# Attention and mixture of experts on one core: the low half of each expert pair's gated product is subtracted on GpSimd instead of VectorE

## Reference

```python
x = layernorm(x + attention(x))     # 16 heads of 16, causal, window of 64
x = layernorm(x + moe(x))
...
g = einsum('th,eih->tei', x, gate_w)      # 16 experts of 128, 4 of them per token
u = einsum('th,eih->tei', x, up_w)
h = silu(g) * u                           # the gated product
yo = einsum('tei,ehi->teh', h, down_w)
routed = einsum('te,teh->th', combine, yo)
out = routed + shared                     # shared: the same MLP, 256 wide, for all tokens
```

## Time and profile before

| what | value |
|---|---|
| median of 3 runs | 1211.92 us (1211.19 to 1212.39) |
| the profiled execution's own time | 1207.38 us |
| its span | 1205.6 us |
| PE busy | 1001.5 us (83%) |
| DVE busy | 857.8 us (71%) |
| ACT busy | 628.5 us (52%) |
| POOL busy | 493.3 us (41%) |
| chain that ended last | PE 49%, DVE 18%, POOL 12%, issue 8%, DMA 5%, SPq 4%, ACT 3% |
| low half on DVE (L1431) | 136 instructions, 63.5 us |
| scatters, gathers on POOL | 128 and 128 instructions, 127.5 and 124.3 us |

### The profile page before, as it was taken

The page is one execution under the profiler, slowest core; times in us unless marked ns, Lnnn a source line. Parts: engine busy times, 40 slices in busy tenths (PEclk is TensorE's granted clock), DMA queues, the critical chain, the costliest instruction groups (busy, mean ns, idle before and its releaser), DMA issues.

```text
span 1205.6 us, 25555 instructions
## 1 busy us (share of the span) xinstructions
PE 1001.5 (83%) x8693; PEld 587.6 (49%) x8693; DVE 857.8 (71%) x1907; ACT 628.5 (52%) x1449; POOL 493.3 (41%) x712
## 2 busy tenths in 40 slices
PE   7976998989887999998899879887998787966950
PEld 3533433345432465555565445454655466845730
DVE  7666897778885667778777887787767659665443
ACT  4413776767444566664466556654565553324430
POOL 7922221133138112312463733213726726663334
PEclk9988998999888999999999899999999988978985
DMA  5843267421113343242285733322756644968952
GB/s 181 269 136 114 57 215 255 153 70 33 50 58 118 88 111 79 55 80 73 87 176 126 179 92 96 66 76 75 158 120 157 187 123 145 204 151 198 231 155 74
DMA packets 221978, 152.85 MB, mean 127 GB/s; under 512 B 139936, under 2 KB 199072, under 8 KB 221856
## 3 DMA queue, kind: packets, MB, share of 16 engines
q1 hardware_dynamic: 207936, 114.50, 37.9%
q0 software_dynamic: 12288, 33.57, 9.0%
q10 hardware_dynamic: 1632, 3.15, 1.0%
HBM read 50.36 MB, written 73.40 MB: 103 GB/s over the span
## 4 chain that ended last, share of the span: by engine, by line
PE 49%; DVE 18%; POOL 12%; issue 8%; DMA 5%; SPq 4%; ACT 3%; DVEq 0%; ACTq 0%; POOLq 0%
PE bank L711 12%; PE bank L566 10%; PE bank L537 8%; PE bank L550 8%; POOL a_pool L1023 5%; DVE a_mx L1203 5%; PE bank L724 4%; POOL rows L1015 3%; DMA a_pool<-outs,e_slot 2%; DVE e_R L1449 2%; SPq L801 2%; PE bank L540 2%; PE bank L736 2%; DVE e_ga L1420 1%; POOL p_qk L948 1%
## 5 line engine op out<-in xcount | busy, mean ns | idle before, releaser
L1203 DVE TENSOR_REDUCE a_mx<-bank 128x1 f32<-128x512 f32 (+3 forms) x720 | 424.4, 619 | 190.0 <-PE bank L540 115.6
L1084 ACT ACTIVATE a_PT<-bank 128x512 f32<-128x512 f32 (+4 forms) x832 | 374.1, 497 | 215.7 <-PE bank L550 212.9
L550 PE MATMUL bank<-a_QS,a_KS 113*128 113x512 f16 (+4 forms) x832 | 276.5, 340 | 34.4 <-DVE a_mx L1203 25.1
L973 POOL TENSOR_SCALAR_AFFINE_SELECT a_PT<-a_PT 128x256 f32<-128x256 f32 (+1 forms) x288 | 110.9, 392 | 432.6 <-ACT a_PT L1084 431.9
L537 PE MATMUL bank<-a_KS,a_QS 112*128 112x512 f16 (+4 forms) x832 | 265.7, 340 | 23.7 <-DMA a_KS<-k_dram 14.0
L566 PE MATMUL bank<-a_PT,a_VG 128*17 128x512 f32 (+4 forms) x1664 | 186.0, 520 | 18.5 <-POOL a_PT L973 18.5
L1023 POOL DMA_INDIRECT a_pool<-outs,e_slot x128 | 124.3, 971 | 84.8 <-issue 33.9
L1015 POOL DMA_INDIRECT rows<-e_XR,e_slot x128 | 127.5, 996 | 66.0 <-issue 35.4
L537 PEld LDWEIGHTS bank<-a_KS,a_QS 112*128 112x128 f16 x832 | 81.4, 100 | 126.1 <-ACT a_PT L1084 51.1
L550 PEld LDWEIGHTS bank<-a_QS,a_KS 113*128 113x128 f16 x832 | 82.3, 100 | 100.9 <-DVE a_mx L1203 40.8
L1149 ACT ACTIVATE e_tq<-bank 128x256 f32<-128x256 f32 x136 | 51.0, 382 | 145.6 <-PE bank L711 145.5
(11 more groups left out here) (156 smaller groups left out, 1263.2 us busy)
## 6 DMA issues: line engine op xcount, KB each, us to landing
outs<-e_ys SPq DMA_DIRECT2D x104, 256.0 KB
rows<-a_pool SPq DMA_DIRECT2D x48, 256.0 KB, 3.2
q_dram<-p_qk SPq DMA_DIRECT2D x32, 128.0 KB, 2.7
k_dram<-p_qk SPq DMA_DIRECT2D x32, 128.0 KB, 2.6
v_dram<-p_vs SPq DMA_DIRECT2D x8, 512.0 KB, 4.2
a_QS<-q_dram SPq DMA_DIRECT2D x64, 64.0 KB
a_KS<-k_dram SPq DMA_DIRECT2D x64, 64.0 KB
a_VG<-v_dram SPq DMA_DIRECT2D x16, 256.0 KB, 4.4
```

What stands on the lines that cost most here:

```text
L550: pe.matmul(ps[:, 0:(qc + 1) * CH - q0], KS[p][0:MR + 1, kt // NT, h % 2, kt % NT * P:kt % NT * P + P], QS[p][0:MR + 1, qc, h, q0 - qc * C ...
L973: pool.affine_select(out=a, in_=a, compare_op=ALU.is_ge, fill=0.0, base=q0 - (kt * P - WIN), pattern=[[0, 2], [1, w]], channel_multiplier= ...
L1084: act.activation(PT[(G + i) % 2][:, h, 0:w], bank("ST", G, i, h)[:, 0:w], ACT.Exp)\
L1203: dve.tensor_reduce(mx[:, piece, t // NT, heads[0]:heads[0] + n, t % NT], bank("S", G, u)[:, 0:n * w].rearrange("p (h k) -> p h k", h=n), ...
```

## The change

The job `hl` of each of the 136 pairs leaves DVE's list and enters POOL's, at the same half-slot `q + 3`. The instruction, its shape, its buffers, its waits and the semaphore it raises stay the same; what it stands behind and in front of is different.

```diff
--- before.py
+++ after.py
@@ -205,7 +205,7 @@
         act[q].append(("tanh", g, n))
         dve[q + 1].append(("gate", g, n))
         act[q + 2].append(("hh", g, n))
-        dve[q + 3].append(("hl", g, n))
+        pool[q + 3].append(("hl", g, n))
         if n >= NPS[g]:
             sp[q - (5 if q < tail + 10 else 10)].append(("load_rows", g, n))
             last[g] = y = put(("y", g, n), q + (5 if q < tail else 7))
@@ -1004,6 +1004,13 @@
                         on.wait_ge(f["row_hi"], c + 1)
                         pool.tensor_tensor(XR[:, j:j + NT, D:2 * D], x1_of(c), XR[:, j:j + NT, 0:D], op=ALU.subtract)\
                             .then_inc(f["row_lo"], 1)
+                    elif what == "hl":
+                        q = nth(*a)
+                        on.wait_ge(f["hh_done"], q + 1)
+                        if q >= NHB:
+                            on.wait_ge(*free_h(q - NHB))
+                        pool.tensor_tensor(hl[q % NHB][:], hf[q % NHF][:], hh[q % NHB][:], op=ALU.subtract)\
+                            .then_inc(f["hl_done"], 1)
                     elif what == "scatter":
                         b, t, k = a
                         on.wait_ge(f["slot_done"], b + 1)
@@ -1423,13 +1430,6 @@
                         on.wait_ge(f["hl_done"], q - NHF + 1)
                         dve.scalar_tensor_tensor(hf[q % NHF][:], ps[:, 2 * P:4 * P], 0.5 / WSC / WSC, ga[q % 2][:],
                                                  op0=ALU.mult, op1=ALU.mult).then_inc(f["h_done"], 1)
-                    elif what == "hl":
-                        q = nth(*a)
-                        on.wait_ge(f["hh_done"], q + 1)
-                        if q >= NHB:
-                            on.wait_ge(*free_h(q - NHB))
-                        dve.tensor_tensor(hl[q % NHB][:], hf[q % NHF][:], hh[q % NHB][:], op=ALU.subtract)\
-                            .then_inc(f["hl_done"], 1)
                     elif what == "add_shared":
                         b, n = a
                         c, tile = shared_place(b, n)
```

## The result

| | before | changed |
|---|---|---|
| median | 1211.56 us (4 runs, 1211.19 to 1212.39) | 1224.72 us (4 runs, 1217.70 to 1230.04) |
| ratio | | 1.0103, 95% interval 1.0062 to 1.0144 |
| the profiled execution's own time, its span | 1207.38, 1205.6 us | 1222.22, 1220.5 us |
| DVE, POOL busy | 857.8, 493.3 us | 814.6, 582.6 us |

The account below looks back on a forecast made before the run. PE was taken to bound half the chain, POOL's transfers the stretch behind the attention; -5 + 12 + 5 + 5 + 2 + 3 + 2 = +24 on 1207.38 gave 1231.4, plus 4.5 to the median: 1236 us, range 1216 to 1256.

Parts of the forecast that it names:

- relief of DVE: 136 subtractions leave DVE; only what lies on the chain counts: -5 us, between 0 and -10.
- scatters of group 1, of group 2: Six low halves each between masks, 4.8 us, less a cover of 2.7: +1.5 us each, +3 together (0 to 6).
- group 0's gathers: Five low halves on POOL, 4.0 us, half of it hidden: +2 us (0 to 4).
- group 1's gathers: Nine low halves between first and last gather, +7.2, partly taken by pauses for combines: +5 us (0 to 8).
- tail, to PE's product behind it: Low halves among group 3's and 4's scatters and group 2's gathers delay PE's next down product: +12 us (0 to 18).
- from there to the end (group 3's gathers): Nine low halves ahead of group 3's gathers and five between them, less pauses for combines: +5 us (2 to 8).
- meeting on SBUF: Low halves on POOL slow DVE's combines; if a sixth meets one in full: +2 us (0 to 10).
- The price of a low half: One low half on POOL takes 0.80 us (bounds 0.62 and 1.0), 109 us in all.
- Stretch from group 4's first scatter to the end of group 2's last gather: Behind the attention: some 79 us instead of 68; forecast wrong if it does not grow by at least 8.
- the third rival: Each stop feeds the next: POOL waits for high halves, late POOL stops DVE's gates; +16 in the tail, 1252 us, chance 0.15.
- the landing loops hide the gathers' share: Pauses for combines in the gather stretches absorb most low halves there: +8, 1220 us, chance 0.15.
- The relief deciding: POOL's landings hide every added low half; PE gains 6 us in the tail plus 5 of relief: 1201 us, chance 0.07.

Follow-up runs that it names:

- the two mirror kernels: Changed kernel with the low halves behind the attention back on VectorE: 1.0005 of the kernel before; with only those on GpSimd: 1.0093.
- the second trace: Profiled execution of the changed kernel run again with nothing edited: 1221.23 us (8 runs), 1.0087 of the kernel before.
- Narrow on GpSimd: Changed kernel with the subtraction cut from 256 to 16 columns in all but the first six pairs: 1203.04 us, 0.9937 of the kernel before.
- the free stretches: Kernel before with only 45 attention pairs' low halves on GpSimd, away from scatters and group 0's and 1's gathers: 1207.94 us, 0.9969.
- all four variants: Against the kernel before: low halves on GpSimd for scatters of groups 3 and 4, 0.9863; from group 2's gathers on, 0.9902; 16 columns on GpSimd, 0.9773; on VectorE, 0.9942.

## Why the prediction was right, and where it was too large

By its own steps, each against the changed kernel's trace (starts from the table):

| step | forecast | shown by the trace |
|---|---|---|
| relief of DVE | -5 | -7.5 |
| scatters of group 1, of group 2 | +1.5, +1.5 | +3.6, +1.4 |
| group 0's gathers | +2 | +1.4 |
| group 1's gathers | +5 | +2.5 |
| tail, to PE's product behind it | +12 | +10.1 |
| from there to the end (group 3's gathers) | +5 | +3.3 |
| meeting on SBUF | +2 | within the others |
| sum | +24 | +14.85 in this trace; 10.5 and 13 by the medians |

The relief is what is left: at group 3's first scatter the kernel was 1.42 late, the four stretches of the attention had cost 8.9, so the rest gave 7.5. The tail is 11.55 at PE's product less that 1.42, the last step 14.85 less 11.55. The rows of the attention are one trace's: the second has 2.1 for the relief, and 3.5, 1.7, 0.5 and 1.9 for the four stretches in the order of the table.

Of the signs, POOL was busy 582.6 us (600 forecast) and DVE 814.6 (795), and group 1's gathers started 0.4 and 1.1 us late in the two traces (within 3 forecast).

- **What bounds the kernel, and where the loss arises: right.** The one stretch in which POOL is the clock is the one that loses, and the two mirror kernels show it: +0.6 us in the attention, +11.3 behind it.
- **The price of a low half: the step that failed in size.** "I take 0.80 us", from the nearest rows of 128x256 and 128x512. It is 0.696 by the group and 0.56 between transfers, since a transfer behind a low half starts after 0.16 and not 0.30. The rows shown had only the 0.30, though the trace of before has the shorter pause behind its masks. With 0.56 the 24 low halves of the tail are 13.4 and not 19.2. A second term was mis-sized the other way: the sum took two pauses back whole, 2.08 and 2.91, and they gave back 1.00 and 1.25 (2.08 became 1.08, 2.91 became 1.66). 13.4 less 2.25 is 11.2, and 11.3 was found; the two errors partly cancel, and that is luck. The Trainium skill's figure (GPSIMD Engine Reference, "Elementwise — side-by-side cycle accounting"), by proportion an estimate of 0.56 for the instruction, was said to make the sum 8 us smaller. The instruction itself took 0.674 in the median, between the Trainium skill's proportion and the 0.80.
- **Stretch from group 4's first scatter to the end of group 2's last gather: 79 forecast, 76.4 found** (1031.21 to 1106.62 + 0.94), 67.9 before; the growth of 8.4 is just over the 8 below which the forecast was to count as wrong. "The last gather ends 14.2 later" became 11.3 (+12.69 less +1.42) and 9.0 in the second trace, whose stretch grew by 6.9 only, under the 8. This sign was at the edge.
- **The path to the down product: right, with one more step behind it.** The two low halves follow the last gather, and the product of the earlier trace rows comes 1.5 behind that gather's end where 3.7 was before and 1.7 forecast. It is 10.49 late, 9.1 of them made since group 3's first scatter. Two products on, PE waited for a gate behind the last combine, which is the loop of the third rival at one place, and that made it 10.1.
- **Group 3's gathers: right in kind.** "Nine stand in front, so the gathers start 2 to 4 later": they are 15.48 late where PE's product was 11.55 late; 3.2 of that is the order of the list. The five between them were 2.8 instead of 4.0, and the pauses for combines took them back: +16.82 at the last of them and +14.85 at group 4's first.
- **Relief of DVE: 7.5 and 2.1 in the two traces**, against 5 and inside its bounds of 0 to 10, so its size stays open. Narrow on GpSimd, 7.6 us under the kernel before, and the free stretches, 3.8 with a third of the pairs, show that there is one.
- **Meeting on SBUF**: the combines took 4.7 us more in all (65.3 to 70.0), where 2 were forecast on the path. They come from low halves: by the timelines of both engines, 18 of the 128 operations lie in time beside a low half on POOL and take 0.84 us in the mean, the other 110 take 0.50, and the low halves they meet take 0.86 to 0.90 in several places instead of 0.67. One in seven meets one, near the sixth of the forecast, but at 0.34 more each. Against that, the 3.62 of the earlier trace rows became 2.76: all four of its operations lay beside additions on POOL before, and only two lie beside a low half or an addition now.
- **The rivals.** That the landing loops hide the gathers' share (1220, 0.15) was nearest in us, but not in kind: the idle time ahead of gathers shrank by 33 us in sum, half of it ahead of group 3's first, and the gathers still cost most. That each stop feeds the next: DVE's gate did wait for low halves, 8.5 us in 6 places, and PE in 26 places, 38.9 us in sum. Narrow on GpSimd still has 6.7 us of the first, and 26.3 in 19 places of the second, and no loss. So this rival's 1252 did not come, and how much of the 13 us runs through such waits stays open. The relief deciding (1201) is what narrow low halves do, and full ones do not.

## What to carry to other kernels

An instruction moved to an engine with 59% idle time cost nothing here where that engine waits for someone, and its full step where the engine's transfers are the clock: list both kinds of stretch before moving, and move only the first kind (here 45 of 136, worth 0.3%, where all 136 cost 1%). Price an added instruction by the step from one neighbour's start to the next, not by its own length, since part of it can go into a pause that was there anyway. In an engine that runs its list in order, look at what each moved instruction stands in front of: nine low halves ahead of a gather made it start behind a cast of a later pair, 3.5 us after its last store had landed. And compare two traces by counting along an engine's list, since the product that looks like the old one can be its neighbour.

## What was not expected of the hardware

**The pause ahead of a transfer on POOL depends on what stands ahead of it.** It is mostly 0.30 behind another transfer and 0.16 behind a low half or a mask, in every kernel here, also with a low half of 0.22 us, and 0.46 or more behind the last small step of a norm (L984). Why it is shorter behind the first two isn't shown.

**A 16-column subtraction takes 0.224 us and a 256-column one 0.674**: 1.9 ns a column with some 0.19 us that don't depend on it (0.224 less 16 x 1.9). The two rows of before that gave the forecast, 1.245 for 512 and 2.133 for 1024 columns, have 1.7 ns a column and 0.36 us beside it; going down from them overshoots at 256.

**The same kernel at 1276.65 and at 1210.79 us on one chip.** In the batch at 1276.65 the trace of the kernel before with narrow low halves on VectorE has waits that no other engine ends (engine, line, releaser: us, times, longest):

```profile
PE bank L712 <- issue: 46.8, 52, 2.7
...
ACT e_tq L1150 <- remote: 90.8, 19, 14.9
```

The kernel before had 3.8 us in 7 places of the first kind, in its trace at 1207.38. Piece by piece it looks like this, on PE and on ACT:

```profile
1072.53 0.37 PE L737 MATMUL bank<-a_W,e_hh 128*128 128x256 f16 x1 [1.70 <-issue]
...
1075.35 0.37 PE L737 MATMUL bank<-a_W,e_hh 128*128 128x256 f16 x1 [2.03 <-issue]
...
1039.32 0.22 ACT L1131 ACTIVATE e_th<-bank 128x64 f32<-128x64 f32 x1 [8.89 <-remote]
```

Single matmuls of one product came 1.5 to 2 us apart, and nothing in the trace ended the wait. Most of the 55 us were lost in the stretches of scatters and gathers: against the kernel before at 1207.38, group 2's gathers took 20.9 us more from first to last (+28.37 to +49.31). In that batch all four variants were faster than the kernel before, also those with low halves on GpSimd, which cost 5 and 10 us elsewhere. So a verdict of 1% here holds only where the kernel before takes some 1210. What that batch met, and why low halves on GpSimd helped in it, was not found out.
